# Layer 1's split expert weights: kept in SBUF for all eight experts and addressed by register, in place of a DRAM copy and a transfer per slot

## What is computed

```python
def _L1_ffn_ref(x, ln1_w, ln2_w, wq, wk, wv, wo, router_w, w1, w2, w3):
    ...                      # attention: 4 heads, 2 key heads, causal
    x = x + y @ wo.T
    flat = _rmsnorm(x, ln2_w).reshape(-1, Cx)
    probs = jax.nn.softmax(flat @ router_w.T, axis=-1)
    tp, ti = jax.lax.top_k(probs, TOPK)
    tp = tp / (jnp.sum(tp, axis=-1, keepdims=True) + 1e-09)
    weights = jnp.sum(tp[..., None] * jax.nn.one_hot(ti, NE, dtype=flat.dtype), axis=1)
    out = jnp.zeros_like(flat)
    for e in range(NE):
        hh = jax.nn.silu(flat @ w1[e].T) * (flat @ w3[e].T)
        out = out + weights[:, e:e + 1] * (hh @ w2[e].T)
    return x + out.reshape(Bx, Tx, Cx)
```

## Time and profile before

| what | us |
|---|---|
| median of 3 runs | 620.7 |
| the runs | 619.45, 620.7, 745.92 |
| the profiled execution | 617.0 |
| its span, first to last instruction | 614.8 |
| mean granted TensorE clock | 0.929 |

### The profile page before, as it was taken

The page is one execution under the profiler, slowest core; times in us unless marked ns, Lnnn a source line. Parts: engine busy times, 40 slices in busy tenths (PEclk is TensorE's granted clock), DMA queues, the critical chain, the costliest instruction groups (busy, mean ns, idle before and its releaser), DMA issues. The chain is left out here.

```text
span 614.8 us, 12091 instructions
## 1 busy us (share of the span) xinstructions
PE 507.4 (83%) x3865; PEld 283.2 (46%) x3865; DVE 433.6 (71%) x1076; ACT 319.9 (52%) x533; POOL 272.5 (44%) x310
## 2 busy tenths in 40 slices
PE   2999986699999799977766887998968768978881
PEld 1533334477777454534322323333412257766770
DVE  6998848978999935576793886998761068545454
ACT  0777986769999001110334544763744465535451
POOL 3000006133436402332183895996444527866542
PEclk9999996999999999997685989999979799989995
DMA  8999954000039340112034221003015145666665
GB/s 302 416 421 422 399 183 161 19 19 20 28 130 410 95 100 0 33 39 76 0 103 103 70 66 23 1 1 81 11 50 168 39 106 167 172 186 184 169 192 164
DMA packets 46086, 81.92 MB, mean 133 GB/s; under 512 B 8112, under 2 KB 37600, under 8 KB 41680
## 3 DMA queue, kind: packets, MB, share of 16 engines
q1 hardware_dynamic: 42304, 76.33, 38.1%
q0 software_dynamic: 2272, 4.69, 2.2%
q10 hardware_dynamic: 1456, 0.22, 0.2%
HBM read 61.72 MB, written 17.11 MB: 128 GB/s over the span
## 5 line engine op out<-in xcount | busy, mean ns | idle before, releaser
L1275 ACT ACTIVATE A<-ps 128x1024 f32<-128x1024 f32 (+3 forms) x80 | 68.6, 893 | 54.4 <-PE ps L1712 42.4
L2358 DVE TENSOR_REDUCE A<-ps 128x1 f32<-128x512 f32 (+3 forms) x160 | 86.1, 602 | 11.5 <-PE ps L1620 10.9
L969 POOL TENSOR_TENSOR G<-G,A 128x1024 f32<-128x1024 f32 (+3 forms) x40 | 73.9, 1890 | 16.8 <-ACT A L1275 16.7
L1369 PE MATMUL ps<-R,G 128*128 128x512 f32 x128 | 59.2, 605 | 1.1 <-DVE G L1920 0.8
L1620 PE MATMUL ps<-A 96*128 96x512 f16 (+3 forms) x160 | 53.5, 373 | 7.4 <-DVE A L2358 4.9
L1543 PE MATMUL ps<-A,G 128*128 128x512 f32 x128 | 59.2, 594 | 0.0
L1823 PE MATMUL ps<-A 128*128 128x128 f16 (+1 forms) x702 | 50.4, 226 | 5.4 <-issue 5.0
L1471 PE MATMUL ps<-R 128*128 128x128 f16 x768 | 48.3, 220 | 6.7 <-DVE x L2038 5.8
L1712 PE MATMUL ps<-A 97*128 97x512 f16 (+3 forms) x160 | 46.3, 375 | 8.1 <-ACT A L1275 8.1
L1471 PEld LDWEIGHTS ps<-R 128*128 128x128 f16 x768 | 45.4, 98 | 14.3 <-issue 6.6
L2020 DVE SCALAR_TENSOR_TENSOR R<-R 128x512 f16<-128x512 f32 x64 | 46.5, 750 | 7.0 <-ACT R L1130 6.8
(11 more groups left out here) (315 smaller groups left out, 948.8 us busy)
## 6 DMA issues: line engine op xcount, KB each, us to landing
A<-in_adj_t SPq DMA_DIRECT2D x16, 1024.0 KB, 17.6
A<-w_split SPq DMA_DIRECT2D x39, 341.0 KB
slots_in<-xn SPq DMA_DIRECT2D x1, 8320.0 KB, 22.4
R<-in_adj_in SPq DMA_DIRECT2D x7, 1024.0 KB, 5.7
xn<-in_adj_in SPq DMA_DIRECT2D x5, 1024.0 KB, 12.9
xT<-in_adj_in SPq DMA_DIRECT2D x4, 1024.0 KB, 12.6
A<-in_f_w SPq DMA_DIRECT2D x16, 170.5 KB
w_split<-A SPq DMA_DIRECT2D x8, 341.0 KB, 5.0
```

The source lines that it names most:

```text
L969: pool.tensor_tensor(total, total, probabilities(n, pair)[:, :, t0:CW], ALU.add).then_inc(s_sum, 1)
L1275: act.activation(probabilities(n, pair)[:, :, t0:CW], ps[:, 2 * pair:2 * pair + 2, t0:CW], ACT.Exp, scale=1.0 / (SQ * SQ * float(HD) ** 0. ...
L1369: last = pe.matmul(ps[:, c, :], G[:, j, :], fbuf[:, j % FB, CW * c:CW * c + CW], start=(j == 0), stop=(j == NT - 1))
L2358: dve.reduce_max(pm[:, h, t % TPC, b:b + 1], ps[:, bank, 0:width], AX_X).then_inc(s_rmf, 1)
```

## The change

- `w_split`, `store_split` and `load_first` are gone. The split w1 and w3 of all eight experts stay in SBUF, as two arrays (`w13[0]` the high parts, `w13[1]` the low parts) over the same eight rows of A.
- The staging places v13 and v2 lie elsewhere in A; w2's copies are strided in three parts. The experts are prepared in the order 6, 7, 0 to 5, at later steps of attention (`PREPARE_AT`, `LOW_AT`); the third may start only when all keys are split (`s_klo`). ScalarE waits for all eight at the end of attention.
- `hidden1` reads the expert's number into a register first, and its weight loads take their address from it. `output1` uses the same register and reads none.
- The rows of slots come in 12 batches, each with its own semaphore, and SyncE issues them one behind the other without a wait for slots used.

```diff
+        v13 = A[:, 14:16, 2 * CW:2 * CW + 2 * H1]
+        v2 = A[:, 6:12, 2 * CW - D:2 * CW].rearrange("p (s k) d -> p s k d", s=2)
...
-        w13_at = [(6, 0), (8, 0), (10, 0), (12, 0), (6, 4 * CW), (8, 4 * CW)]
-        WB = len(w13_at)
-        w13 = [A16[:, j:j + 2, o:o + 2 * H1] for j, o in w13_at]
+        w13 = [A16[:, 6:6 + E1, o:o + 2 * H1] for o in (0, 4 * CW)]
+        PREPARED = (6, 7, 0, 1, 2, 3, 4, 5)
...
-        XB = 6
-        BATCHES = (1, 2, 3, 3, 4, 4, 1, 3, 4, 4, 4, 4, 2)
+        XB = 12
+        BATCHES = (1, 2, 3, 3, 4, 4, 1, 3, 4, 4, 5, 5)
...
-        PREPARE_AT = {(0, 1): 0, (0, 2): 1, (0, 3): 2, (1, 2): 3, (1, 5): 4, (2, 4): 5, (2, 8): 6, (3, 4): 7}
+        PREPARE_AT = {(0, 1): 0, (0, 2): 1, (1, 3): 2, (1, 5): 3, (2, 1): 4, (2, 4): 5, (2, 8): 6, (3, 4): 7}
...
-        LOW_AT = {(0, 1): 0, (0, 2): 1, (1, 0): 2, (1, 2): 3, (1, 5): 4}
+        LOW_AT = {(0, 1): 0, (0, 2): 1, (1, 4): 2, (1, 6): 3, (2, 2): 4}
...
+            def load_expert1(n):
+
+                s, e = n % 2, PREPARED[n]
+                if n >= 2:
+                    sp.wait_ge(s_wlo, n - 1)
...
+            load_expert1(4)
+            load_expert1(5)
             stack_row_max(2)
+            load_expert1(6)
             stack_row_max(3)
...
-                if b >= XB:
-                    sp.wait_ge(s_sT, ENDS[b - XB])
...
-            for n in range(WB):
-                load_first(n)
             sp.wait_ge(s_negT, NC)
             sp.wait_ge(s_od, NC - 1)
-            for b in range(4):
+            for b in range(len(BATCHES)):
                 load_slot_rows(b)
-            b = 4
-            for n in range(WB, SLOTS):
-                load_first(n)
...
             def hidden1(n):
 
-                pe.wait_ge(s_w13l[n % WB], AGAIN + 16 * (n // WB + 1))
+                g = 0 if n < FIRST else 1
+                i = n - IDS[g][0]
+                if n == 0:
+                    pe.wait_ge(s_wlo, E1)
+                if i == 0:
+                    pe.wait_ge(s_route, EXPERTS_KNOWN[g])
+                expert[n] = pe.value_load(expert_i[g][0:1, i:i + 1], min_val=0, max_val=E1 - 1)
                 pe.wait_ge(s_sxl, n + 1)
...
-                            last = pe.matmul(ps[0:w, bank + n % 2, P * k:P * k + P], w13[n % WB][:, part, o:o + w], a,
+                            last = pe.matmul(ps[0:w, bank + n % 2, P * k:P * k + P], w13[part][:, bass.ds(expert[n], 1), o:o + w].rearrange("p a w -> p (a w)"), a,
...
             def output1(n):
 
-                e = pe.value_load(expert_i[g][0:1, i:i + 1], min_val=0, max_val=E1 - 1)
+                e = expert.pop(n)
```

More of the change, by code:

```diff
@@ L47 @@
 RW = D + 2
-W13 = 4 * H1
 W2C = 2 * 3 * D
@@ L263, in program @@
         assert len(homes) == SLOTS and ROWS_AT + 10 * RW <= 4 * T
-        XB = 6
-        BATCHES = (1, 2, 3, 3, 4, 4, 1, 3, 4, 4, 4, 4, 2)
+        XB = 12
+        BATCHES = (1, 2, 3, 3, 4, 4, 1, 3, 4, 4, 5, 5)
         ENDS = [sum(BATCHES[:b + 1]) for b in range(len(BATCHES))]
-        assert ENDS[5] == FIRST and ENDS[-1] == SLOTS
+        assert len(BATCHES) == XB and ENDS[5] == FIRST and ENDS[-1] == SLOTS
         batch_of = [b for b, count in enumerate(BATCHES) for _ in range(count)]
@@ L459, in program @@
         AGAIN = 16
-        s_xr, s_w13l = [*s_A[0:4], s_A[10], s_A[15]], s_A[4:4 + WB]
-        assert len(s_xr) == XB and WB <= 6
+        s_xr = [*s_A[0:11], s_A[15]]
+        assert len(s_xr) == XB
         s_squares, SQUARES = s_first, 16 * 3
@@ L729, in _ @@
             sp.wait_ge(s_made, 3)
-            load_expert1(0, 0)
-            load_expert1(1, 1)
-            store_split(0)
+            load_expert1(0)
+            load_expert1(1)
+            load_expert1(2)
             stack(2, True)
-            store_split(1)
+            load_expert1(3)
             stack(2, False)
             stack_row_max(1)
-            store_split(2)
             stack(3, True)
             stack(3, False)
-            store_split(3)
-            store_split(4)
+            load_expert1(4)
+            load_expert1(5)
             stack_row_max(2)
+            load_expert1(6)
             stack_row_max(3)
[L744 to L758, removed]
-                sp.dma_start(w13[n % WB], w_split[bass.ds(e, 1), :, :].rearrange("a p (n w) -> (a p) n w", n=2)
-                             ).then_inc(s_w13l[n % WB], 16)
+            load_expert1(7)
             blocks_in = slots_in.rearrange("(b p) w -> b p w", p=P)
@@ L995, in _ @@
                     clear_sums(c)
-                if (c, turn) == (1, 0):
-                    low_weights(LOW_AT[(1, 0)])
                 add_to_sums(n)
@@ L1795, in rows_there @@
             def rows_there(b):
-                return AGAIN + 16 * sum(BATCHES[b % XB:b + 1:XB])
+                return AGAIN + 16 * BATCHES[b]
             def slot_transpose(n):
-                pe.wait_ge(s_xr[batch_of[n] % XB], rows_there(batch_of[n]))
+                pe.wait_ge(s_xr[batch_of[n]], rows_there(batch_of[n]))
                 if n == 0:
@@ L1807, in slot_transpose @@
                 pe.transpose(ps[:, x_bank(n), 0:P], slot_rows(n)[:, 0:D], ident[:, :]).then_inc(s_sT, 1)
+            expert = {}
             def hidden1(n):
-                pe.wait_ge(s_w13l[n % WB], AGAIN + 16 * (n // WB + 1))
+                g = 0 if n < FIRST else 1
[5 more added lines that the diff above has]
+                expert[n] = pe.value_load(expert_i[g][0:1, i:i + 1], min_val=0, max_val=E1 - 1)
                 pe.wait_ge(s_sxl, n + 1)
```

60 lines of the change are left out of this document (22 added, 38 removed).

## The result

The kernel after the change takes 648.36 us (median of 4 runs, 644.9 to 650.5), the kernel before 620.7 us (median of 3 runs, 619.45 to 624.62; a fourth, of 745.92 us, stands apart and is left out): ratio 1.044, 95% interval 1.039 to 1.049. The forecast was 645 us, with a range of 631 to 661. The profiled run took 650.5 us, span 648.5, against a span of 614.8 before: +33.7 us.

What follows compares the result with a forecast made beforehand. TensorE, busy 83% of the span, was taken as the bound, its sequencer pacing the new expert loop. 617.0 + 25.0 (loop) + 0.6 (slots 0 and 1) = 642.6, with the median's offset 645 us; range 631 to 661.

Steps and rivals of the forecast that it cites:

- The bound and what is removed: Expert loop: TensorE is the busiest engine; the 39 weight transfers and eight stores removed are not what ends a wait last.
- The loop: Expert loop, 36 turns growing from 2.67 to 3.36 us each: +25 us, with all old stalls vanishing under the longer turn.
- transpose and chain: Start of each expert-loop turn: transpose 0.10 us, then the exposed register chain 0.87 us.
- hidden products with the wait step: Each expert-loop turn: hidden products 1.46 us, then a wait step of 0.20 us ahead of the output products.
- the register read moves: Each expert-loop turn: the read, now ahead of the hidden products, is no longer covered by queued matmuls: +0.8 us.
- the twelve register instructions: Hidden products of each turn: addresses from registers slow 18 weight-load pairs to 81 ns each, 1.46 us for 1.02: +0.44 us.
- Rivals 1 and 2: Expert loop: 1, register work stays beside the array, 611 us, chance 0.06; 2, arithmetic costs, read hidden, 620 us, 0.07.
- One low part into chunk 2: Attention: GpSimd's added work ends at 420.55, TensorE needs its sums at 423.38, so just hidden; 0 us taken, -2 to +3.
- One sign of being wrong: Start of the loop: slot 2's hidden products more than 4 us later than 501.10 would point to the attention stage.
- The +0.6 us for slots 0 and 1: First two slots: slot 1 adds 1.24 us, 0.76 of it beside a wait; slot 0's addition lies beside a wait.
- The end: From the start of the last hidden products to the end: unchanged, about 18 us.
- The rival of the falling clock: Expert loop at half clock: turn 4.2 us, 675 us if throughout, 660 if for half of the loop; chance 0.13.

Runs made afterwards that it cites:

- run 8: Kernel before with only the first six of 39 weight transfers; later slots use what lies in the buffers: 618.58 us, ratio to before 0.996.
- run 1: Kernel after with the next slot's register read moved behind the hidden products: 634.25 us on a faster chip, ratio to the kernel before 1.052.
- run 12: Kernel before with the register read moved in front of the hidden products: 626.84 us, ratio to the kernel before 1.001.
- run 2: Kernel after with all hidden products at a fixed weight address, the read left in front: 595.53 us, ratio to the kernel before 0.987.
- run 9: Kernel after with half of the hidden products (9 of 18) at a fixed address, six register instructions fewer: 626.23 us, ratio to before 1.002.
- run 4: Kernel after with each expert's number read into a register twice: 659.07 us, ratio to the kernel before 1.094.
- the second pair: Kernels before and after, unchanged, measured and profiled again on one other chip: 623.69 and 647.95 us, ratio of after to before 1.041.
- run 11: Kernel before with GpSimd's low parts 5 and 6 waiting for VectorE's first routing steps: 625.41 us, ratio to the kernel before 0.9998.
- run 10: Kernel after with one load for six experts' numbers, no assertion, and GpSimd's low parts 5 and 6 behind VectorE's first routing steps: 632.37 us, ratio to before 1.008.
- run 3: Kernel after with hidden products at fixed addresses and the register read back behind them: 592.31 us, ratio to the kernel before 0.985.
- run 7: Kernel after with GpSimd's low parts 5 and 6 waiting for VectorE's first routing steps: 645.19 us, ratio to the kernel before 1.037.

## Why the prediction was right, and where it was not

**The bound and what is removed: right in kind.** The weights of a slot were nobody's last wait; run 8 puts 33 of their transfers at 2.6 us (0.2 to 5). All stalls of the old loop were let go under the longer turn, and so it came: no row of slot rows or transfers is left among TensorE's waits.

**The loop: right in sum, 25.0 against 25.8 us.** By its parts, in the turn from 578.12: transpose and chain 0.97 forecast, 0.91 measured; hidden products with the wait step 1.66 forecast, 1.63 measured; output products 0.73 and 0.74. The turn was 3.36 forecast and 3.38 on average.

**But the split by cause was wrong.** The step was "the register read moves ... I take +0.8 us for each turn", with +0.44 for the twelve register instructions. Undoing the move alone gives back 0.00 us (run 1), making it alone in the kernel before costs under 0.1 (run 12). Taking the twelve instructions away alone gives back 1.4 us of the shortest turn (3.26 to 1.87 in run 2, where the array becomes the limit), six of them 0.70 (run 9), where 24 ns for each of nine pairs would have been 0.22. They are the whole cause of the longer turn: at some 0.12 us each they make the sequencer's turn (3.3 us) longer than the array's 1.9, and a read that had been free, 0.64 us (run 4), becomes as dear as everything else that the sequencer does. The prediction did say that the sequencer would pace the new turn, and added up the new turn's parts rightly. What it had wrong is what each of them would give back. That the sum came out is in part luck: I took the exposed read from a turn in which the sequencer happened to be late (579.0 in the earlier trace rows), and that is the state of every turn now. Rivals 1 and 2 fell with it: neither the read nor the arithmetic is hidden.

**Attention and slots 0 and 1: the sizes were off.** "One low part into chunk 2 ... is just hidden" was argued for TensorE's sums, and for them it is true: the last sums are taken 0.24 us later than before (424.05 against 423.81). The step overlooked who else runs beside GpSimd: VectorE's routing operation was held 2.4 us longer, and that cost 1.6 to 3 us. One sign of being wrong that the prediction gave, slot 2's hidden products more than 4 us late, came true: they were 10.1 us late (7.4 in the second pair), where it allowed 0.6. The +0.6 us for slots 0 and 1 was 1.9 us, and both slots ran at half the clock (497 to 510.6 us):

```profile
508.29 2.13 PE L1799 MATMUL ps<-A 128*128 128x128 f16 x18
```

where the kernel before had 1.17 us for slot 1. In run 8, a kernel before whose slots 0 and 1 ran at half clock, they take 1.3 us more than in its first profile, so most of the 1.9 us is the clock. The greater part of the delay lies in the passage into the loop: from the last exp of attention (484.4 us in the kernel before) to slot 2 it is 16.7 us in the two profiles of the kernel before and 23.9 and 24.2 in those of the kernel after, 7.2 and 7.5 us more. But runs 8, 11 and 12, which leave the front of the kernel before nearly untouched, need 19.0, 21.6 and 24.2 us with 14 to 21 us of half clock there. So the register addresses alone don't explain it, and what grants or denies the clock in this passage stays open. Nor does one profile tell how often it happens: run 11 shows this passage 5 us longer than the kernel before, and its median is the same. That the two profiled runs of the kernel before, 617.0 and 620.4 us, were without it and lay below their medians fits this. For the same reason the 10.1 us should not be added to the loop's 25.8: between the medians lie 27.7 us (26.8 on the second chip), where the forecast had 24.3. The loop makes up nearly all of it.

**The end: not unchanged but 2.3 us shorter.** No experiment was made on this. Over all profiles it is 15.3 to 15.8 us where the turn is 2.8 us or longer, and 16.4 to 17.8 where it is shorter, as if a slower loop left less unfinished behind it; that is not shown.

**The rival of the falling clock** did not come in the loop of this kernel (1.00 from 510.6 to 640.3 us); it came at 4.02 us a turn (run 4), not at 3.38. Its price was too high as well: the rival added the register chain to products at half clock, 4.2 us a turn, which with a second read would be 4.8, and run 4's turns in its stretches of half clock were 3.9 to 4.3. The 1.92 and 0.96 us in that sum are the steps between the groups' starts in the earlier trace rows, at a clock of 0.50.

## What to carry to other kernels

A register address was not free in this loop of 28 short matmuls a turn: each instruction that makes an operand's address (12 for 18 weight loads) cost TensorE's sequencer 0.12 us and each read of a register 0.64 us, so add them over a turn and compare the sum with the array's own time. In the kernel before, with six such instructions a turn and by the same count a sum of some 1.8 us (an estimate: 3.28 less twelve times 0.124), moving the read cost under 0.1 us a turn (run 12). In the kernel after, where the sum was above the array's 1.9 us, one more read was paid in full (+0.64, run 4), six instructions fewer gave 0.70 us back and twelve 1.4 (runs 9 and 2), reading less often, though the read had been there before, 0.45 (run 10), and moving the read about changed nothing (run 1). Replacing transfers that nobody waited for could not pay for this: without the addresses' price the change was worth some 11 us (run 3), and the addresses cost more than twice that.

When work moves from one stretch to another on GpSimd, look at VectorE's operations in that stretch as well as at who waits for the result: here one with both inputs in SBUF, 0.19 us by itself, took 5.62.

## What the runs showed of the hardware that was not expected

- A VectorE operation of 0.19 us lasted 5.62 us beside GpSimd's subtractions, and ended 0.06 us behind the last of them. Both of its inputs, R and sm, lie in SBUF. Not held were the reduction just ahead of it, with the one input R (422.06 in the kernel after, 0.19 us beside GpSimd's sum), and the operation at 429.48 in run 7, with an input in PSUM: 0.69 us beside GpSimd's subtraction, and 0.69 again at 432.99, with nothing on GpSimd. The first was held longer than one instruction: past the end of the sum that ran when it started (423.22) and through four subtractions that followed without a pause, all of which started after it. In the kernel before (3.17 us, to 425.22) and in run 7 (0.95 us, to 423.37) it ended as well 0.05 us behind GpSimd's run of instructions (425.17 and 423.32), so in these three traces the length of the run is what counts.
- The pace of a group of matmuls says little of the group: output products with the same six register instructions ran at 82 ns a pair in the kernel after and at 61 in run 2, hidden products with them at 84 ns in the kernel after and at 58 in run 9.
- Six registers loaded at once took 1.5 us in four cases and 0.86 us in one, five took 0.60 us, where one takes 0.30.
- A register instruction that is shown as 46 ns long took 0.124 us of TensorE's sequencer, with one or two weight loads beside it.
- The kernel before took 603.7, 621.2 and 625.6 us on three chips, 3.6% between the lowest and the highest, more than most single edits here, so times are compared here only between kernels on one chip.
